# Keeping the plain lanes of the window build in DRAM for the second layer, in place of comparing again

## What is computed

```
h = relu(layernorm(x)); x = x + L0(h, edge_index)               # 3 hops of normalised sums
h = relu(layernorm(x)); x = x + L1(h, edge_index, edge_weight)  # weighted convolution
h = relu(layernorm(x)); x = x + L2(h, src, dst)                 # mean of neighbours
h = relu(layernorm(x)); x = x + L3(h, edge_attr, src, dst)      # message network

# L1, where the change lies (no self loops but those in src/dst and one of weight 1 per node)
deg  = segment_sum(w, col);  dinv = rsqrt(deg) where deg > 0
norm = dinv[row] * w * dinv[col]
out  = segment_sum((x @ W)[row] * norm[:, None], col);  return relu(out + b)
```

## Time and profile before

| | us |
|---|---|
| median of 3 runs | 1075.51 (1074.43 to 1076.52) |
| the profiled execution | 1078.87 |
| its span, first to last instruction | 1077.1 |
| PE busy | 921.8 (86%) |
| VectorE busy | 827.8 (77%) |
| ScalarE busy | 450.3 (42%) |
| POOL busy | 574.0 (53%) |

### The profile page before, as it was taken

One profiled execution on the slowest core, in us unless ns is written; L12 is line 12 of the kernel. 1 busy time (PEld: TensorE's weight loads), 2 busy tenths in 40 slices (PEclk: granted clock), 3 DMA queues, 4 the chain that ended last, 5 costly groups with the idle time before them and its releaser, 6 DMA issues.

```text
span 1077.1 us, 23987 instructions
## 1 busy us (share of the span) xinstructions
PE 921.8 (86%) x6195; PEld 584.2 (54%) x6195; DVE 827.8 (77%) x2585; ACT 450.3 (42%) x879; POOL 574.0 (53%) x747
## 2 busy tenths in 40 slices
PE   3788888699977777877789859999999999999995
PEld 2466665355535556666565535555555555555563
DVE  8988888743569788898876776777777787777776
ACT  2577777310005454544421234444434434434431
POOL 6533433000015777777710067777777777777770
PEclk9677777899988999999889969999999999999997
DMA  3000000610002111111126165544544545445441
GB/s 66 2 1 0 0 0 0 229 70 1 1 0 47 26 26 27 27 26 27 27 87 189 27 173 116 115 103 107 108 101 104 109 98 105 109 100 105 102 92 33
DMA packets 144600, 72.30 MB, mean 67 GB/s; under 512 B 111661, under 2 KB 136442, under 8 KB 144410
## 3 DMA queue, kind: packets, MB, share of 16 engines
q1 hardware_dynamic: 127224, 54.98, 19.5%
q0 software_dynamic: 15936, 16.35, 8.6%
q10 hardware_dynamic: 1378, 0.22, 0.1%
HBM read 59.13 MB, written 12.35 MB: 66 GB/s over the span
## 4 chain that ended last, share of the span: by engine, by line
PE 44%; DVE 21%; POOL 13%; issue 10%; ACT 5%; DMA 4%; DVEq 2%; ACTq 1%; SPq 1%; POOLq 0%
PE seg L1627 9%; POOL A L1221 7%; POOL pair L1221 6%; PE seg L1812 6%; PE big L1848 5%; PE big L1557 5%; ACT A L1356 4%; DVE A L1974 3%; PE big L1838 3%; PE seg L1859 3%; PE seg L1880 3%; PE seg L1571 2%; DMA A<-table,src_i 1%; DVE A L1963 1%; DVE acc_mem L1985 1%
## 5 line engine op out<-in xcount | busy, mean ns | idle before, releaser
L1221 POOL DMA_INDIRECT A<-table,src_i x338 | 323.1, 956 | 114.7 <-issue 97.5
L1221 POOL DMA_INDIRECT pair<-table,src_i x160 | 162.2, 1013 | 62.1 <-issue 48.5
L1356 ACT CAST A<-big 128x500 f32 x208 | 125.4, 603 | 48.1 <-PE big L1562 26.8
L1812 PE MATMUL seg<-A 128*128 128x384 f16 (+1 forms) x624 | 121.4, 338 | 11.9 <-DVE A L2040 8.2
L1471 ACT COPY A<-big 128x512 f32<-128x512 f32 x104 | 60.8, 584 | 121.3 <-PE big L1838 119.7
L1848 PE MATMUL big<-A 128*128 128x512 f32 x208 | 109.8, 610 | 0.5 <-DMA A<-pr_table 0.5
L1477 ACT ACTIVATE A<-big,A 128x512 f32<-128x512 f32 x104 | 71.5, 688 | 92.0 <-PE big L1849 92.0
L1671 PE MATMUL big<-A 128*128 128x300 bf16 (+1 forms) x512 | 93.8, 328 | 16.5 <-DVE A L1963 15.7
L1812 PEld LDWEIGHTS seg<-A 128*128 128x128 f16 x624 | 57.4, 99 | 91.2 <-issue 36.7
L1284 POOL COPY cur<-pair 128x24 bf16 x100 | 40.2, 446 | 94.6 <-PE seg L1571 94.6
L2074 DVE TENSOR_TENSOR A<-seg,A 128x448 f32<-128x448 f32 x78 | 48.7, 624 | 47.5 <-PE seg L1815 29.6
(11 more groups left out here) (321 smaller groups left out, 1734.2 us busy)
## 6 DMA issues: line engine op xcount, KB each, us to landing
A<-in_edge_attr_dram SPq DMA_DIRECT2D x103, 128.0 KB
A<-drel_flat SPq DMA_DIRECT2D x104, 126.0 KB
spilled_adjacency<-A SPq DMA_DIRECT2D x1, 7074.0 KB, 21.8
A<-spilled_adjacency SPq DMA_DIRECT2D x6, 1152.0 KB, 9.9
A<-table,src_i POOLq DMA_INDIRECT x338
A<-pr_table SPq DMA_DIRECT2D x104, 31.5 KB
pair<-table,src_i POOLq DMA_INDIRECT x160
A<-low_flat SPq DMA_DIRECT2D x78, 32.0 KB, 3.1
```

The costliest lines, as they stand in the source:

```text
L1221: pool.indirect_dma_start(out=row, out_offset=None, in_=table, in_offset=bass.IndirectOffsetOnAxis(ap=src_i[:, tile:tile + 1], axis=0)).th ...
L1356: nc.scalar.copy(A[:, :, bass.ds(bases[k], PW)], big[:, k % 4, 0:PC].rearrange("p (s d) -> p s d", d=PW)).then_inc(window_kept, 1)
L1812: op = nc.tensor.matmul(made[:, 0:held.shape[2] * D], hot_low[:, u, m, :], held[:, k, :, :], start=(m == 0 and k == 0), stop=(m == 3 and k ...
```

## The change

In the build SyncE stores every half's plain lanes to a new DRAM tensor, `lanes_kept`, as soon as `lanes_ready` says that they are there. VectorE, before it writes a lanes buffer again, waits for the stores from it (`lanes_moved`, one semaphore a buffer). In the second layer `lanes1` becomes two buffers, one for each half of a block; SyncE loads the lanes of half blocks into them, each load when the multiplication of the half block before that in the same buffer is done, and `weighted_lanes` waits for the load and multiplies. The second buffer takes the room of `mantissa`, so the first load into it waits until the mantissas are split. SyncE waits for all stores before it reloads `x`, ScalarE for those of two buffers before it uses their room.

```diff
+        lanes_kept = nc.dram_tensor("lanes_kept", [2 * ITB, P, 8 * P], F16, kind="Internal").ap()
...
-        lanes1 = carve1(4 * P).bitcast(F16).rearrange("p (v k) -> p v k", k=8)
+        lanes1 = [carve1(4 * P).bitcast(F16) for _ in range(2)]
...
-        mantissa = carve1(T)
+        mantissa = lanes1[1].bitcast(F32)[:, 0:T]
...
+        lanes_moved = [sem(f"lanes_moved{h}") for h in range(4)]
...
+            def store_lanes(it, odd):
+                for half in range(2):
+                    sp.wait_ge(lanes_ready, it * 2 + (half + 1))
+                    sp.dma_start(lanes_kept[bass.ds(it * 2 + half, 1), :, :].rearrange("a p e -> p (a e)"),
+                                 hot_l[2 * odd + half].rearrange("p v k -> p (v k)")).then_inc(lanes_moved[2 * odd + half], 16)
+
+            store_lanes(0, 0)
+            store_lanes(1, 1)
+            with sp.Fori(1, ITB // 2) as two:
+                store_lanes(two * 2, 0)
+                store_lanes(two * 2 + 1, 1)
+
+            def load_lanes(b, half):
+                if b:
+                    sp.wait_ge(lanes_ready, (b + ITB) * 2 + (half - 1))
+                sp.dma_start(lanes1[half], lanes_kept[T1 // 8 + 2 * b + half, :, :]).then_inc(lanes_moved[half], 16)
+
+            for h in range(4):
+                sp.wait_ge(lanes_moved[h], ITB // 2 * 16)
             sp.wait_ge(window_kept, PAIRS + 4)
...
+            sp.wait_ge(ev("spilled"), 16)
+            sp.wait_ge(ev("sums_ps"), 3 * ROUNDS)
+            load_lanes(0, 0)
+            sp.wait_ge(ev("weights_split"), 1)
+            load_lanes(0, 1)
+            for b in range(1, NB):
+                for half in range(2):
+                    load_lanes(b, half)
+
             sp.wait_ge(ev("applied"), NB)
-            sp.wait_ge(ev("spilled"), 16)
...
+            for h in range(2):
+                act.wait_ge(lanes_moved[h], ITB // 2 * 16)
             for n in range(3):
                 copy_sums(n)
...
                 dve.wait_ge(window_built, it * PS + (5 + 4 * h))
-                same_as(lanes1, key_l[:, tiles], P, 8).then_inc(ev("lanes_plain"), 1)
-                dve.wait_ge(ev("lanes_plain"), b * 2 + (h + 1))
+                dve.wait_ge(lanes_moved[h], (b + 1 + ITB // 2) * 16)
                 for m, part in enumerate((mantissa_hi, mantissa_lo)):
-                    op = dve.tensor_tensor(hot_l1[:, h, m, :, :], lanes1,
+                    op = dve.tensor_tensor(hot_l1[:, h, m, :, :], lanes1[h].rearrange("p (v k) -> p v k", k=8),
...
                     if turn >= 2:
                         dve.wait_ge(window_built, it * PS + (4 * half - 3))
+                        dve.wait_ge(lanes_moved[h], it * 8 - 8 * odd)
                     same_as(hot_l[h], key_l[:, bass.ds(it * (2 * PS) + 8 * half, 8)], P, 8)
...
             link(dve.tensor_tensor(mantissa_lo, mantissa, mantissa_hi, ALU.subtract))
+            dve.sem_inc(ev("weights_split"), 1)
```

More of the change, by code:

```diff
@@ L2443 @@
           "neigh_out": "h_parts_ready", "acc_cleared": "rows2_read", "deg_ps": "chooser_ready", "pads": "sums_cleared",
-          "sum_ps0": "node_weights_ready", "sum_ps1": "node_steps", "ld_w": "picked", "fills": "rows_16_ready", "h_L2": "src_low_ready", "ld_x": "x_cleared", "sum_ps3": "squares0"}
+          "sum_ps0": "node_weights_ready", "sum_ps1": "node_steps", "ld_w": "picked", "fills": "rows_16_ready", "h_L2": "src_low_ready", "ld_x": "x_cleared", "sum_ps3": "squares0",
+          "idx_ready0": "lanes_moved0", "idx_ready1": "lanes_moved1", "idx_ready2": "lanes_moved2", "idx_ready3": "lanes_moved3"}
 def build(nc, *args):
```

## The result

The changed kernel takes 1079.37 us (median of 20 runs, 1075.99 to 1082.38), the kernel before 1076.76 us (20 runs, 1074.43 to 1079.74). The ratio is 1.0028 with a 95% interval of 1.0017 to 1.0039: **slower by 0.28%, some 3 us, where 9 us less were forecast**. The profiled execution is 1081.62 us with a span of 1079.8; before it was 1078.87 and 1077.1.

What follows compares the result with a forecast made beforehand. VectorE was taken to end the second layer's weighted build, with the gathers close behind as a floor. 8.2 + 2.0 - 0.4 - 0.8 = 9.0 us off the median of 1075.5 gave 1066.5 us, range 1063.5 to 1071.5.

Steps and rivals of the forecast that it cites:

- Stores in the build: Build: 52 stores of 256 KB land in 3.2 to 5.2 us, within 11.8 us of cover, and cost 0.
- Rival (d): Build: stores don't land within 11.8 us, VectorE waits for its buffer; slower, about 1092 us; chance 0.08.
- End of the stage: Weighted build, second layer: without the comparisons gathers pace it, and PE finishes the last block 8.2 us earlier.
- its last hots of block 14 need PE's window of the step behind group 35: End of weighted build: VectorE can't run far ahead of PE, whose window there is done at 525.5 us.
- Shorter gathers: Weighted build: POOL's gathers stretch less without 32 comparisons beside them; 2.0 us gained, with ends 0 and 3.9.
- Loads in the second layer: Second layer: the first load may hold up the table's store, 0.4 us; a load may delay a gather's landing, 0.8 us.
- The prediction's own signs of error: Wrong if VectorE idles on a load or store, gathers start later than 332.5, or the stage still ends on VectorE.
- rival (c): Second layer: first load makes all gathers slip 3 us or more, landings later too; nothing measurable, 1073.4 to 1077 us; chance 0.06.

Runs made afterwards that it cites:

- e1: Changed kernel with the second layer of the kernel before, so the build's 52 stores stay and nothing is loaded; 1.0069 of the time before.
- e3: Changed kernel with each iteration's first-half store issued after ScalarE's register load instead of across it; 0.9976 of the time before, 1074.72 us.
- e10: Kernel before with 30 of the 32 plain comparisons of the second layer left out and nothing in their place; 0.9951 of the time before.
- e2: Changed kernel with 48 of the 52 stores left out and the 32 loads kept; 0.9970 of the time before.
- e6: Kernel before with only VectorE's norm of the early nodes moved behind the second step of block 15; 1.0014 of the time before.

## Why the prediction was wrong, step by step

- **Stores in the build, "covered, 0": this step failed, and with it the sign.** It asked one question, whether a store lands before VectorE writes its buffer again, and answered it rightly: landing in 2.0 us (3.2 to 5.2 estimated), 11.8 us of cover, no wait. What it left out is whom a store slows while it moves. ScalarE's register load was on the build's chain (2.5% of it before, 5.2% after), but no group of busy time shows it, and the prediction took the build's spare time from VectorE's idling alone. It cost 5.5 us (the last one-hot at 196.4 us in e1, at 190.8 in e3).
- **Rival (d)** had the right side by luck, with the wrong mechanism and size: 3 us slower instead of some 17, without one wait of VectorE for a store.
- **End of the stage, 8.2 us: the term was mis-sized.** Counted from the first gather, the last block begins at 544.02 - 7.09 = 536.9, where 535.2 was forecast, and its four steps take 11.7 us (544.02 to 555.7), where 10.0 were. The step that failed is "its last hots of block 14 need PE's window of the step behind group 35": those hots (533.86) wait for nothing. The last thing VectorE waits for in block 14 is PE's window for the second half's lanes (527.89), and from there 16.1 us of its own queue follow, of which the sum counted 9.7. For the same reason PE idles ahead of the last block as before and takes its first row at 2.53 us, which the sum left out.
- **Shorter gathers, 2.0 us: nothing of it came out.** The mean went from 1013 ns to 1004, 1.4 us in all, and in e10, with 30 comparisons gone, it is 1013 as before; the gathers don't end the stage either. By the Trainium skill's rule ("SBUF — State Buffer", "Who interferes with whom") this term was 0, and that is how it came out. The rule's reason is not borne out: all gathers over 1.3 us in the changed kernel lie beside products, the longest at 2.27 us, though another beside two products took 0.94:

```profile
347.23 0.94 POOL L1250 DMA_INDIRECT pair<-table,src_i  x1 [0.30 <-issue]
...
351.18 2.27 POOL L1250 DMA_INDIRECT pair<-table,src_i  x1 [0.30 <-issue]
```

- **Loads in the second layer, 0.4 + 0.8:** the first load made VectorE wait 3.7 us and delayed nothing on the path (POOL waited 13.72 us for the table, 13.68 before), and the later landing of the pacing gather, 0.7 us, was estimated about right, though the stage is no longer for it than in e10 (215.8 against 215.9).
- **What no step had:** the hops' first sweep took 10.12 us instead of 8.68, and the first gather slipped by 1.5 us more than the build. The granted clock was 0.79 in the 16 us from 200 on before, and 0.63 in the 16 us from 205 on after; e2, with the build of before, has 0.70 and 0.8 us of it. But e6 and e10 have the whole build and the hops of before, without a store, and this row takes 8.82 us in e6 (clock 0.72) and 10.07 us in e10 (0.68):

```profile
205.64 10.07 PE L1627 MATMUL seg<-A,acc_mem 128*128 128x512 f16 x33 [7.67 <-DVEq L2205]
```

So it varies by as much between executions, and the 1.5 us are not shown to come from the change. Why PE is at the lower of its two levels (1.2 and 2.4 GHz) for longer in some of them stays open.

- **The prediction's own signs of error were good ones:** the stage still ending on VectorE (it does) and an iteration of 6.3 us (157.6 us over 24 intervals, 6.57). Gathers starting later than 332.5 (338.96) is a blunter sign: e10, with nothing added, starts them at 333.21. Together, in the two profiled executions: 5.5 + 1.5 lost, 5.1 won, 0.8 later at the end, where no cause was looked for: 2.7 us slower.
- **Two slips in side sums** that the forecast doesn't rest on: from 423.89 to 539.00 there are 16 comparisons, both ends counted, not 15; and rival (c)'s gain of 2.8 us makes 1072.7, not 1073.4.

## What to carry to other kernels

Ask of every added transfer not only who waits for it, but what runs beside it while it moves. Register loads are the first to look at: they show as ACTq, DVEq or POOLq in the chain of waits and in no list of busy time, and here one grew by half beside a 256 KB store. Where it can't be kept from the path, issue the store behind it: one moved wait turned a loss of 0.28% into a gain of 0.24%. And when work is taken out of a queue, walk that queue to the end with the waits that are left: behind its last wait for another engine, every instruction still counts.

## What the runs showed of the hardware

- A register load of eight values by ScalarE takes 0.547 us and up to 1.08 us beside stores, one by POOL 0.318 and up to 0.639. The one of ScalarE read closely, at 124.2 us, ended at 125.1, when the store's bytes had just about moved.
- What decides in the main is which partitions the store reads: with the loaded row on the first partition and stores from 0 to 63, POOL's median is 0.459 us; from 64 to 127, 0.321. That the row could be put on a partition of the other half instead was not tried.
- The price depends on whether loads and stores meet: in six kernels with slightly later or longer stores, most of ScalarE's loads ended up in the gaps between them (medians 0.547 to 0.549 us), and half, the same and twice the bytes cost the build 0.2 to 1.2 us where the change cost 5.5.
